# Last feed-forward of a four-layer transformer kernel: the row norm moves from VectorE to GpSimd, and so does the factor of the second rounding

## The reference, cut to what matters

```
def rmsnorm(x):
    return x * rsqrt(mean(x * x, axis=-1) + 1e-5)
def act_quant(x):
    scale = 127.0 / clip(max(abs(x), axis=-1), 1e-5)
    return clip(round(x * scale), -128.0, 127.0) / scale
def bitlinear(x, w, b):
    return einsum('bsd,fd->bsf', act_quant(rmsnorm(x)), weight_quant(w)) + b
h = bitlinear(x, w1, b1)          # 256 -> 1024
h = gelu(h)
return bitlinear(h, w2, b2)       # 1024 -> 256
x = x + _L3_ffn_ref(_layernorm(x), ...)
```

## Time and profile before

| | |
|---|---|
| median of 3 runs | 1873.37 us (1869.57 to 1875.02) |
| the profiled execution's own time | 1867.5 us |
| its span, first to last instruction | 1865.7 us |
| mean granted TensorE clock | 0.926 of full |
| busy over the span: PE, DVE, ACT, POOL | 86%, 57%, 48%, 20% |
| busy from 1800 to 1820 us: PE, DVE, ACT, POOL | 13.83, 19.46, 15.37, 8.28 of 20.00 us |

### The profile page before, as it was taken

One profiled execution on the slowest core, in us unless ns is written; L12 is line 12 of the kernel. 1 busy time (PEld: TensorE's weight loads), 2 busy tenths in 40 slices (PEclk: granted clock), 3 DMA queues, 4 the chain that ended last, 5 costly groups with the idle time before them and its releaser, 6 DMA issues.

```text
span 1865.7 us, 27946 instructions
## 1 busy us (share of the span) xinstructions
PE 1601.8 (86%) x10002; PEld 1223.1 (66%) x10002; DVE 1066.6 (57%) x3010; ACT 898.6 (48%) x2022; POOL 380.5 (20%) x472
## 2 busy tenths in 40 slices
PE   6999854999679999999858799999998679994666
PEld 5677654888556767667536666777766668894544
DVE  7767641222356766666567665555555434325887
ACT  4888811222136666666549355555553002233366
POOL 1000013111132332333240100000001332224734
PEclk9999966999889999999979899999998689997879
DMA  9000037988500000000000200000000338993001
GB/s 337 2 1 2 1 96 267 299 288 291 173 1 12 7 6 7 7 1 1 1 1 1 79 12 6 6 6 7 1 1 12 134 132 258 305 348 108 0 12 34
DMA packets 61625, 152.26 MB, mean 82 GB/s; under 512 B 8960, under 2 KB 39696, under 8 KB 55248
## 3 DMA queue, kind: packets, MB, share of 16 engines
q1 hardware_dynamic: 54096, 133.91, 21.7%
q0 software_dynamic: 5280, 14.47, 2.0%
q10 hardware_dynamic: 2112, 2.10, 0.4%
HBM read 133.89 MB, written 24.75 MB: 85 GB/s over the span
## 4 chain that ended last, share of the span: by engine, by line
PE 68%; DVE 15%; POOL 5%; ACT 5%; issue 4%; DMA 2%; POOLq 0%; SPq 0%; DVEq 0%; ACTq 0%
PE bank L963 8%; PE bank L919 8%; PE bank L1373 8%; PE bank L1427 6%; PE bank L1440 6%; PE bank L1414 5%; PE bank L1377 5%; PE bank L1357 3%; PE bank L659 3%; POOL sorted_h L1153 2%; PE bank L675 2%; PE bank L1776 2%; PE bank L690 1%; ACT p1f L1495 1%; PE bank L933 1%
## 5 line engine op out<-in xcount | busy, mean ns | idle before, releaser
L1624 DVE TENSOR_REDUCE small<-bank 128x1 f32<-128x512 f32 x128 | 82.5, 686 | 108.7 <-PE bank L1427 108.7
L982 ACT ACTIVATE e2a<-bank,WB 128x128 f32<-128x128 f32 x156 | 44.5, 368 | 184.4 <-PE bank L963 184.4
L1620 DVE CUSTOM_DVE_ANT_0 p1f<-bank,p1f 128x512 f32<-128x512 f32 x128 | 83.2, 687 | 81.0 <-PE bank L1427 81.0
L1498 ACT ACTIVATE p2f<-bank,small 128x512 f32<-128x512 f32 x128 | 86.8, 683 | 86.2 <-DVE small L1624 86.2
L731 ACT ACTIVATE l<-l,small 128x256 f32<-128x256 f32 x256 | 108.9, 502 | 32.6 <-DVE small L797 32.2
L1495 ACT ACTIVATE p1f<-p1f,small 128x512 f32<-128x512 f32 x128 | 91.2, 713 | 67.5 <-DVE small L1620 67.2
L380 POOL TENSOR_SCALAR rs<-mv 128x4 f32<-128x4 f32 x20 | 4.5, 227 | 566.7 <-DVEq L230 551.6
L1373 PE MATMUL bank<-WA,HT 128*128 128x256 f32 x384 | 94.2, 389 | 5.0 <-DVE p1f L1565 5.0
L797 DVE CUSTOM_DVE_ANT_0 l<-bank,small 128x256 f32<-128x256 f32 x256 | 90.8, 421 | 13.3 <-PE bank L675 12.4
L982 ACT ACTIVATE e0a<-bank,WB 128x128 f32<-128x128 f32 x128 | 36.5, 368 | 120.8 <-PE bank L963 120.8
L1509 ACT ACTIVATE p2f<-bank 128x512 f32<-128x512 f32 x128 | 75.1, 598 | 40.6 <-PE bank L1414 39.1
(11 more groups left out here) (389 smaller groups left out, 3941.7 us busy)
## 6 DMA issues: line engine op xcount, KB each, us to landing
WB<-in_L2pack SPq DMA_DIRECT2D x39, 514.0 KB, 5.0
WB<-in_L2pack SPq DMA_DIRECT2D x39, 512.0 KB, 5.5
WB<-in_L0pack SPq DMA_DIRECT2D x16, 1028.0 KB, 6.1
WB<-in_L0pack SPq DMA_DIRECT2D x16, 1024.0 KB, 6.4
e0a<-in_L0pack SPq DMA_DIRECT2D x7, 1028.0 KB, 6.3
e0a<-in_L0pack SPq DMA_DIRECT2D x7, 1024.0 KB, 7.0
sorted_h<-in_blank SPq DMA_DIRECT2D x6, 1032.0 KB, 16.6
e2a<-sorted_h SPq DMA_DIRECT2D x39, 129.0 KB, 5.4
```

The costliest lines, as they stand in the source:

```text
L1498: ins = a.e.activation(P, k.bank(x), ACT.Exp, bias=self.mx[:, m:m + 1], accum_out=self.sm[:, m:m + 1])
```

## The change

- For tiles 4 to 15 the norm of the row goes to GpSimd, as a step `xr` with lag -18, three times ahead of VectorE's largest magnitude, which keeps its lag -15. The row of tiles 0 to 3 stays on VectorE, ahead of the fence.
- VectorE's `fac` is gone. GpSimd's `pow` makes the factor: it multiplies the inverse root by 127 (L2430 of the new kernel), makes `cut` and the output's scale as before (L2432, L2433), takes `cut` to the power -1/2 (L2434), and multiplies this root by itself and by the scaled inverse root (L2435), which raises the semaphore that `rndh` waits for.
- The semaphore between GpSimd's `pow` and VectorE's `fac` is gone; two groups of columns in `small` (`hscl`, `hroot`) take the place of one (`hinv`).

```
-    AT = (("x", -15), ("cut", -14), ... ("pow", 7), ("fac", 8), ("rndh", 9), ...
+    AT = (("xr", -18), ("x", -15), ("cut", -14), ... ("pow", 7), ("rndh", 9), ...
 early_dv:
         for i in range(4):
             self.row(v, i)
+            self.largest(v, i)
-    def row(self, v, i):
+    def row(self, s, i):
         k, x = self.k, self.xs[i % 8]
+        s.wait_ge(self.rn, i // 4 + 1)
+        s.wait_ge(self.xtr, i - 7)
+        s.e.tensor_scalar(x, k.X[:, i, :], k.mv[:, i, 0:1], k.rs2[:, i:i + 1], ALU.subtract, ALU.mult).then_inc(self.xn.sem, 1)
+
+    def largest(self, v, i):
+        x = self.xs[i % 8]
         v.wait_ge(self.xn, i + 1)
         v.e.tensor_reduce(self.xtop[:, i:i + 1], x, AX.X, ALU.max, apply_absolute_value=True).then_inc(self.xtops.sem, 1)
 dv:
             if s == "x" and i > 3:
-                self.row(v, i)
+                self.largest(v, i)
-            elif s == "fac":
-                v.wait_ge(self.pow, i + 1)
-                v.chain(e.reciprocal(self.hinv[:, i:i + 1], self.hcut[:, i:i + 1]))
-                e.tensor_scalar(self.hfac[:, i:i + 1], self.hinv[:, i:i + 1], self.hss[:, i:i + 1], 127.0, ALU.mult, ALU.mult).then_inc(self.fac.sem, 1)
 po:
+            if s == "xr" and i > 3:
+                self.row(g, i)
             elif s == "pow":
                 g.chain(g.e.tensor_scalar(r, r, 1.0 / 1024, eps, ALU.mult, ALU.add))
                 g.chain(g.e.tensor_tensor(r, r, k.nhalf[:, 0:1], ALU.pow))
+                g.e.tensor_scalar(self.hscl[:, i:i + 1], r, 127.0, None, ALU.mult)
                 g.wait_ge(self.top, i + 1)
                 g.chain(g.e.tensor_scalar(cut, self.htop[:, i:i + 1], r, 1e-5, ALU.mult, ALU.max))
-                g.e.tensor_scalar(self.hout[:, i:i + 1], cut, ...).then_inc(self.pow.sem, 1)
+                g.e.tensor_scalar(self.hout[:, i:i + 1], cut, ...)
+                g.chain(g.e.tensor_tensor(self.hroot[:, i:i + 1], cut, k.nhalf[:, 0:1], ALU.pow))
+                g.e.tensor_scalar(self.hfac[:, i:i + 1], self.hroot[:, i:i + 1], self.hroot[:, i:i + 1], self.hscl[:, i:i + 1],
+                                  ALU.mult, ALU.mult).then_inc(self.fac.sem, 1)
```

More of the change, by code:

```diff
@@ L2196 @@
 class Layer3Ffn(Beside):
-    AT = (("x", -15), ("cut", -14), ("rnd", -3), ("tx", -2), ("ex", -1), ("up", 3), ("deq", 4), ("gelu", 5), ("sq", 6), ("top", 6),
-          ("pow", 7), ("fac", 8), ("rndh", 9), ("th", 10), ("eh", 11), ("down", 12), ("y", 13), ("add", 14))
+    AT = (("xr", -18), ("x", -15), ("cut", -14), ("rnd", -3), ("tx", -2), ("ex", -1), ("up", 3), ("deq", 4), ("gelu", 5), ("sq", 6), ("top", 6),
+          ("pow", 7), ("rndh", 9), ("th", 10), ("eh", 11), ("down", 12), ("y", 13), ("add", 14))
     def __init__(self, k):
@@ L2217, in __init__ @@
         st = k.small[:, 128:384].rearrange("p (s t) -> p s t", s=16)
-        self.xtop, self.xinv, self.xout, self.hss, self.htop, self.hcut, self.hinv, self.hfac, self.hout = (st[:, i, :] for i in range(9))
+        self.xtop, self.xinv, self.xout, self.hss, self.htop, self.hcut, self.hscl, self.hroot, self.hfac, self.hout = \
+            (st[:, i, :] for i in range(10))
         k.stat_of["f3"] = self.stat = k.flag("n_stat", 4)
@@ L2227, in __init__ @@
         self.hd, self.gel, self.sqr, self.top = f("f3_h", n), f("gel", n), f("f3_sqr1", n), f("f3_top1", n)
-        self.pow, self.fac, self.hrnd = f("f3_rsd1", n), f("f3_inv1", n), f("f3_rnd1", n)
+        self.fac, self.hrnd = f("f3_inv1", n), f("f3_rnd1", n)
         self.htr, self.hev = f("f3_tr1", n), f("f3_ev1", n)
@@ L2299, in factor @@
         g.e.tensor_tensor(rs, rs, k.nhalf[:, 0:4], ALU.pow).then_inc(self.rn.sem, 1)
-    def row(self, v, i):
+    def row(self, s, i):
         k, x = self.k, self.xs[i % 8]
-        v.wait_ge(self.rn, i // 4 + 1)
-        v.wait_ge(self.xtr, i - 7)
-        v.e.tensor_scalar(x, k.X[:, i, :], k.mv[:, i, 0:1], k.rs2[:, i:i + 1], ALU.subtract, ALU.mult).then_inc(self.xn.sem, 1)
+        s.wait_ge(self.rn, i // 4 + 1)
[3 more added lines that the diff above has]
+        x = self.xs[i % 8]
         v.wait_ge(self.xn, i + 1)
@@ L2421, in po @@
         for i, s in self.walk():
-            if s == "pow":
+            if s == "xr" and i > 3:
+                self.row(g, i)
+            elif s == "pow":
                 r, cut = self.hss[:, i:i + 1], self.hcut[:, i:i + 1]
@@ L2426, in po @@
                 g.chain(g.e.tensor_tensor(r, r, k.nhalf[:, 0:1], ALU.pow))
+                g.e.tensor_scalar(self.hscl[:, i:i + 1], r, 127.0, None, ALU.mult)
                 g.wait_ge(self.top, i + 1)
                 g.chain(g.e.tensor_scalar(cut, self.htop[:, i:i + 1], r, 1e-5, ALU.mult, ALU.max))
-                g.e.tensor_scalar(self.hout[:, i:i + 1], cut, self.sc[:, 6:7], 1.0 / 127.0, ALU.mult, ALU.mult).then_inc(self.pow.sem, 1)
+                g.e.tensor_scalar(self.hout[:, i:i + 1], cut, self.sc[:, 6:7], 1.0 / 127.0, ALU.mult, ALU.mult)
+                g.chain(g.e.tensor_tensor(self.hroot[:, i:i + 1], cut, k.nhalf[:, 0:1], ALU.pow))
+                g.e.tensor_scalar(self.hfac[:, i:i + 1], self.hroot[:, i:i + 1], self.hroot[:, i:i + 1], self.hscl[:, i:i + 1],
+                                  ALU.mult, ALU.mult).then_inc(self.fac.sem, 1)
             elif s == "add":
```

## The result

The changed kernel takes 1885.61 us (median of 4 runs, 1883.29 to 1888.0) against 1872.97 us: a ratio of 1.0066, 95% interval 1.0051 to 1.0080. Taken again beside other kernels it was 1.0048, interval 1.0029 to 1.0068. It is slower by half a per cent or a little more; the forecast was 1877.2 us, 0.2% slower, and its range ended at 1883.

A forecast was written before the change was run, and what follows sets the result against it. VectorE (19.46 of 20.00 us busy) and a two-tile loop through GpSimd bound the kernel. Added time of +2.55 by tile 3, +1.75 by tiles 7 and 11, +3.8 at the end gave 1877.2 us; whole range 1870 to 1883.

The forecast's parts named there:

- The price of a row: Norm of one 128x256 row on GpSimd: 0.75 us, taken near the add; bounds 0.5 and 1.1.
- GpSimd stays under the loop: GpSimd's queue of tiny steps, add, row and hold by a rounding: 4.4 us a tile, under the loop's 4.75.
- The start: Stage start: three reductions wait for GpSimd's rows, so `deq` of tile 0 comes 2.7 us late.
- the tiny part: GpSimd's small steps making the factor: 2.58 us a tile; from first instruction to rounding 2.68, 0.62 longer than before.
- The rival that had GpSimd become the bound: GpSimd's queue sets the pace at 3.63 + row a tile, from a 1.1 us row; +6.8 us, 1880.2; chance 0.13.
- Tiles 3 to 7: Mid-stage, two loop turns of 9.50 us: 19.0 against 19.81, bringing the added time from +2.55 to +1.75.
- tiles 7 to 11: Mid-stage, turns of 9.33 and 9.16 us: 18.5 against 18.51, added time staying at +1.75.
- The loop: Two-tile dependency loop through VectorE, ScalarE and GpSimd: a turn grows from 8.14 to 9.16 us, 9.50 with row magnitudes.
- the collision: GpSimd's add, begun 0.08 before VectorE's rounding, holds it at the shared port: 0.40 us lost; bounds 0 and 0.65.
- Tiles 11 to 15: Tail of the stage: two turns each 1.02 us longer, bringing the added time to +3.8 us.
- Behind the last rounding: Stage end after tile 15's rounding: nothing changes.
- The one of the clock: Rival: TensorE idles longer at the start, its clock rises later and dips longer around 1830; +2 us, 1879.4; chance 0.10.

The follow-up runs named there:

- e9: Changed kernel with rows of tiles 4 to 7 on VectorE and the output scale last, behind the product that releases the rounding; stage 88.74 us.
- e6: Changed kernel, GpSimd's row reduced to one operation for tiles 4 to 15 (mean subtracted, no multiplication by the inverse root); 0.91 us a row.
- e5: Changed kernel with all rows on VectorE, factor on GpSimd, output scale last, behind the product releasing the rounding; 1.0007 against the kernel before, stage 86.44 us.
- e3: Changed kernel with the rows of tiles 4 to 7 back on VectorE; 1.0039 against the kernel before, stage 92.06 us.
- e2: Changed kernel with all rows back on VectorE, only the factor on GpSimd; 1.0024 against the kernel before, stage 91.63 us.
- e4: Changed kernel with two cures: rows of tiles 4 to 7 and all factors on VectorE; 0.9978 against the kernel before, 1.0001 when repeated.
- e1: Changed kernel with the factor back on VectorE, rows still on GpSimd; 1.0011 against the kernel before, stage 89.34 us.

## Why the prediction was wrong

- **The price of a row, and with it the claim that GpSimd stays under the loop: the step that failed.** I took 0.75 us for the row, by the add of the same shape, and named 1.1, the conversion from bytes, as the far end. The row costs 1.21, beyond both. The conversion, a tensor_scalar like the row, was a better neighbour than the add, and even it was short. The page of the Trainium skill "GPSIMD Engine Reference" ("Engine selection") has one-input operations roughly at line rate; my estimate by that was 0.5, and the runs speak against it with 0.91 for the simplest form tried.
- **The start.** The mechanism was as foretold: three reductions wait, and `deq` is late. It was 4.06 us late, not 2.7; three rows by 0.46 are the 1.4 between. By tile 3's rounding 4.27 were lost where I had 2.55.
- **GpSimd stays under 4.75 a tile: wrong.** I had 4.4. It needed 2.83 for the tiny part, 0.71 for the add, 1.67 for the row and 0.09 behind it: 5.30. Of the 0.9 between, 0.46 is the row's price, 0.25 the tiny part (2.58 forecast), 0.16 the hold of the row by a rounding (0.46 for 0.3), and 0.09 the step behind the row, which I had at nothing; the add was 0.04 cheaper. The rival that had GpSimd become the bound was right in kind, and e9 shows it. I gave it 0.13. Its price, 3.63 and the row, was 0.46 short by the same terms, and it said that GpSimd decides from a row of 1.1 us on, while in e6 it does at 0.91. Tiles 3 to 7 brought +1.4 where I had -0.8, tiles 7 to 11 +0.6 where I had 0.
- **The loop, its tiny part and the collision: right, a little low.** In the changed kernel GpSimd's first tiny instruction at 1823.14 releases the rounding at 1826.05, 2.91 us later; in the tail it is 2.88. The forecast was 2.68, so the link grew by 0.82 to 0.85, not 0.62 (the steps behind the first power, without a wait, were 0.32 and 0.22 where I had 0.20 each, the final product 0.38 with its signal). The rounding loses 0.45, forecast 0.40: it was let in 0.19 before the add's recorded end (1820.75 + 1.20 - 0.75 = 1821.20, the add's end 1821.39). Tiles 11 to 15 lost 2.5 us, forecast 2.0; a tile there takes 4.67 us, where the prediction looked for 4.6. The Trainium skill ("SBUF — State Buffer", section on the two separate sides) has whoever starts first hold the shared ports for the whole instruction, with the other fully blocked. For adds e5 agrees from both sides as to who waits. The hold did not last to the add's recorded end, and for rows the recorded start did not decide (last section).
- **Behind the last rounding: nothing changes, I said.** It took 1.35 us longer: 0.45 for the held last rounding, which I forgot at this place, and the rest at TensorE, whose clock was low around 1871 to 1877. The window of 1870 to 1880 in the changed kernel:

```profile
1870.00:1880.00 10.00, 6.36 (x32) 4.95 (x32) 4.39 (x5) 3.66 (x7) 4.43 (x10) 0.66 0.00 0
```

- **The chances.** The rival with GpSimd as the bound came true. The one of the clock did not as I told it: tiles 1 to 3 took 10.9 us, not more than before, and the low clock that cost time came at the end. The forecast of 3.8 was short by 6.4 us: 1.7 at the start, 2.2 in tiles 3 to 7 (0.55 a tile over the loop's 4.75), 0.6 in tiles 7 to 11, 0.5 in the tail and 1.35 behind it, of which some 0.9 is the clock. What the row's price alone is worth can be estimated from e6: a row cheaper by 0.30 brought tile 15's rounding 1.7 us forward, so 0.46 are about 2.7 of the 6.4 us. The rest is the other terms.

## What to carry to other kernels

Look for the price of an operation that moves to GpSimd at rows of the same operation before rows of the same type: over 128x256, two arithmetic operations with operand columns took 1.21 us, an add of two tensors 0.73. When work leaves the bounding engine, add up the whole period of the engine that receives it, with what its neighbours hold it for, and look at what stands ahead of its first result at the stage's start. And where a signal releases a pass that shares ports with the signaller's own next instruction, put something short and harmless between the signal and that instruction: the same arithmetic in another order was worth 3.0 to 3.5 us up to the last rounding here (e3 against e9, e2 against e5).

## What the runs showed of the hardware

Who goes first at the port is not told by the recorded starts alone. An add of GpSimd held the rounding wherever it began just before it, by 0.07 to 0.08 us in the changed kernel, by 0.01 to 0.04 in e5, and it was held itself where it began 0.15 us or more behind. A row of two operations that began 0.05 before a rounding was held (row at 1799.77, rounding at 1799.82 and 0.75 long; the row took 1.76 instead of 1.21):

```profile
1799.77 1.76 POOL L2307 TENSOR_SCALAR WB<-X,mv,rs 128x256 f32<-128x256 f32 x1
```

With one operation (e6), a row that began 0.07 before the rounding and the rounding both lost, 0.36 and 0.20 us:

```profile
1798.74 1.27 POOL L2426 TENSOR_SCALAR WB<-X,mv 128x256 f32<-128x256 f32 x1
...
1798.81 0.95 DVE L2410 TENSOR_SCALAR WB<-WB,small 128x1024 f32<-128x1024 f32 x1 [0.85 <-POOL small L2437]
```

In one tile of e4 a row that began 0.50 before the rounding did not hold it at all (rounding 0.75, row 1.49 instead of 1.23). Why adds and rows differ here, no run shows. Where the VectorE pass was plainly held, the hold ended before the GpSimd instruction's recorded end: 0.19 us for the add, 0.20 for a row of e1 that began 0.83 before the rounding and lasted 1.24, and 0.25 in the stage before.

The last stage's length repeats to within 0.2 us from execution to execution of one kernel where the clock does not differ (86.16 twice, 96.34 and 96.54), while the roughly 1780 us before it scatter by several. The version with both cures, with the low clock at its end for a longer and a shorter time, differed by 1.1 (84.67 and 85.73), and by 0.3 at tile 15's rounding. For effects of this size the stage's own trace is the better instrument than the total, and the start of its last rounding a better one than its end.
